# Scale rows and the later softmax-sum rows through DRAM instead of TensorE transposes

## The reference

```
f  = b[:, ::2, ::2]                       # 40 x 40 positions, 64 channels
w  = 3x3 patches of f                     # L = 1600 patches of 576 values
wn = w / max(norm(w), 1e-4)
y  = einsum('pd,ld->lp', w, wn) * mm      # 1600 x 1600 scores; mm is 1 where the mask patch is 0
y  = softmax(10 * y, axis = l) * mm
out = fold(einsum('lp,ld->pd', y, 4x4 patches of b)) / 4
```

## Time and profile before

| what | value |
|---|---|
| time, median of 3 runs | 1434.59 us (1431.02 to 1434.99) |
| time of the profiled execution | 1435.39 us |
| its span, first to last instruction | 1433.6 us |
| PE busy | 1327.2 us, 93% of the span |
| DVE busy | 1183.3 us, 83% |
| ACT busy | 857.9 us, 60% |
| DMA packets on SP's queue (q1) | 140.50 MB, 41.7% of 16 engines' span |
| mean granted PE clock | 0.983 |

### The profile page before, as it was taken

The page is one execution under the profiler, slowest core; times in us unless marked ns, Lnnn a source line. Parts: engine busy times, 40 slices in busy tenths (PEclk is TensorE's granted clock), DMA queues, the critical chain, the costliest instruction groups (busy, mean ns, idle before and its releaser), DMA issues.

```text
span 1433.6 us, 24384 instructions
## 1 busy us (share of the span) xinstructions
PE 1327.2 (93%) x7190; PEld 894.6 (62%) x7190; DVE 1183.3 (83%) x2827; ACT 857.9 (60%) x2233; POOL 46.9 (3%) x62
## 2 busy tenths in 40 slices
PE   4988999999999899999999899999999999998886
PEld 4756765676556665577656676567655766566433
DVE  3667889799888898889897888979987898978983
ACT  2677646676557565586565764666655855658331
POOL 1000000010000100001000000001000010000100
PEclk9997999999999999999999999999999999999998
DMA  5502482145822556135741359224572236313442
GB/s 91 89 1 85 109 173 76 47 116 119 163 64 67 124 113 150 49 86 127 143 117 33 104 118 179 70 52 110 126 156 67 71 107 135 94 32 96 131 136 53
DMA packets 180471, 142.54 MB, mean 99 GB/s; under 512 B 119859, under 2 KB 177267, under 8 KB 180339
## 3 DMA queue, kind: packets, MB, share of 16 engines
q1 hardware_dynamic: 180178, 140.50, 41.7%
q10 hardware_dynamic: 160, 0.49, 0.2%
HBM read 19.76 MB, written 13.11 MB: 23 GB/s over the span
## 4 chain that ended last, share of the span: by engine, by line
PE 54%; DVE 15%; ACT 11%; issue 8%; SPq 7%; DMA 5%; DVEq 0%; POOL 0%; ACTq 0%; POOLq 0%
PE psO L521 26%; PE psG L471 23%; SPq L326 4%; DVE G L968 4%; ACT S L697 4%; DVE Z L1001 3%; DMA SH<-G 3%; PE psG L480 3%; DVE S L898 3%; ACT G L708 2%; ACT G L683 2%; DVE G L979 2%; DMA SHJ<-G 2%; SPq L270 1%; ACT SQ L624 1%
## 5 line engine op out<-in xcount | busy, mean ns | idle before, releaser
L521 PE MATMUL psO<-Z,B 123*128 123x492 f32 (+2 forms) x1792 | 718.6, 530 | 46.0 <-DVE Z L1001 31.4
L521 PEld LDWEIGHTS psO<-Z,B 123*128 123x128 f32 x1792 | 325.8, 194 | 247.6 <-issue 133.8
L471 PE MATMUL psG<-LH,HL 128*123 128x246 f16 (+2 forms) x2616 | 407.2, 285 | 3.7 <-ACT G L670 3.0
L697 ACT ACTIVATE S<-S,nm 123x480 f32<-123x480 f32 (+3 forms) x560 | 308.5, 555 | 161.2 <-DVE nm L905 160.8
L471 PEld LDWEIGHTS psG<-LH,HL 128*123 128x123 f16 x2616 | 277.4, 137 | 125.4 <-issue 64.5
L708 ACT ACTIVATE G<-G,nb 123x492 f32<-123x492 f32 (+1 forms) x448 | 265.0, 639 | 60.3 <-DVE G L968 59.9
L898 DVE CUSTOM_DVE_ANT_0 S<-G,RB 123x492 f32<-123x492 f32 (+1 forms) x448 | 268.4, 604 | 25.8 <-ACT G L683 15.6
L979 DVE TENSOR_TENSOR G<-G,SH 123x492 f32<-123x492 f32 (+1 forms) x448 | 247.6, 591 | 48.9 <-DMA SH<-G 48.3
L968 DVE SCALAR_TENSOR_TENSOR G<-G,RA,psB 123x492 f32<-123x492 f32 (+1 forms) x448 | 270.4, 647 | 0.0
L883 DVE TENSOR_TENSOR G<-G,psG 123x492 f32<-123x492 f32 (+2 forms) x272 | 135.0, 496 | 90.4 <-PE psG L471 46.5
L1001 DVE TENSOR_TENSOR Z<-G 123x984 f32<-123x984 f32 (+2 forms) x192 | 197.2, 1028 | 0.0
(11 more groups left out here) (79 smaller groups left out, 575.8 us busy)
## 6 DMA issues: line engine op xcount, KB each, us to landing
SH<-G SPq DMA_DIRECT2D x336, 214.8 KB
SH<-G SPq DMA_DIRECT2D x112, 89.2 KB
SH<-G SPq DMA_DIRECT2D x336, 19.2 KB
XP<-x SPq DMA_DIRECT2D x20, 280.0 KB, 5.7
XP<-mid SPq DMA_DIRECT2D x20, 280.0 KB, 5.5
HL<-LH SPq DMA_DIRECT2D x16, 246.5 KB, 4.5
mid<-OSB SPq DMA_DIRECT2D x48, 80.0 KB, 2.3
out<-OSB SPq DMA_DIRECT2D x48, 80.0 KB, 2.3
```

What stands on the lines that cost most here:

```text
L471: last = pe.matmul(psG[0:TW, bank, b0 * TW:b1 * TW], st[:, v % 2, p:p + TW], mv[:, v % 2, lo:lo + n], start=i == 0, stop=i == len(terms) - 1)
L521: last = pe.matmul(psO[:, b, 0:n], B[:, o:o + 128], Z[:, 2 * (s % 2) + j, 0:n], start=t == 0, stop=t == TILES - 1)
L697: last = act.activation(y, y, ACT.Exp, bias=nm[:, k * TILES + t:k * TILES + t + 1], accum_out=sg[:, c:c + 1])
```

## The change

Only unit 0's first 8 scale blocks and the first 8 log-sum-exp blocks of each unit (groups 0 and 1) are still spread by PE. All else is written to DRAM as one row and read back with the source row repeated for 123 partitions.

- For the scales of unit w: PE transposes the 123 x 14 column once (slot 22), ACT copies the 14 x 123 result to `RT` (slot 23), SP writes it to `scale_row` in DRAM (slot 24) and reads it back onto 123 partitions in four DMAs, one for each score chunk: chunks 0 and 1 in slots 26 and 28, chunks 2 and 3 in slots 4 and 10 of the next body.
- For the last 6 log-sum-exp blocks of unit u: one transpose (slot 2), one ACT copy to `LT` (slot 2), a DRAM write (slot 3), one DMA of 123 x 738 into the new SBUF tile `LB` (slot 5). The arguments of chunks 2 and 3 then read `LB` in place of `psB`.
- Unit 0's two remaining spreads go to different banks. DVE no longer makes the separate column `R`.

```diff
+            def write_scales(w):
+                sp.wait_ge(scales_copied, w + 1)
+                sp.dma_start(scale_row[w].rearrange("(t p) -> t p", p=TW), RT[:, :]).then_inc(scales_out, 16)
+            def load_scales(w, k):
+                t0, n = S_CHUNKS[k]
+                if w == 0:
+                    if t0 + n <= RFIRST:
+                        return
+                    n, t0 = t0 + n - max(t0, RFIRST), max(t0, RFIRST)
+                else:
+                    sp.wait_ge(max_made, (w - 1) * NB + (k + 1) * TILES)
+                    sp.sem_inc(sp_gate, 1)
+                sp.wait_ge(scales_out, (w + 1) * 16)
+                row = scale_row[w:w + 1, t0 * TW:(t0 + n) * TW]
+                sp.dma_start(RB[:, t0 * TW:(t0 + n) * TW], row.to_broadcast([TW, n * TW])).then_inc(scales_in[k], 16)
+            def write_lse(u):
+                sp.wait_ge(lse_copied, u + 1)
+                sp.dma_start(lse_tail[u].rearrange("(t p) -> t p", p=TW), LT[:, :]).then_inc(lse_out, 16)
+            def load_lse(u):
+                sp.wait_ge(arg_made, u * NB)
+                sp.sem_inc(sp_gate, 1)
+                sp.wait_ge(lse_out, (u + 1) * 16)
+                sp.dma_start(LB[:, :], lse_tail[u:u + 1, :].to_broadcast([TW, LTAIL * TW])).then_inc(lse_in, 16)
 ...
                     if at and at[2] == 0:
                         shift_strip(at)
+                    if s == FIRST and u is None:
+                        write_scales(v)
+                    if s == 3 and u is not None:
+                        write_lse(u)
+                    if s == 5 and u is not None:
+                        load_lse(u)
+                    if s in (4, 10) and v is not None:
+                        load_scales(v, 2 if s == 4 else 3)
+                    if s == 24 and w is not None:
+                        write_scales(w)
+                    if s in (26, 28) and w is not None:
+                        load_scales(w, 0 if s == 26 else 1)
                     if s in (10, 11, 12) and w is not None:
                         lay_out_features(w, (("HL", "H1", "HV")[s - 10],))
 ...
+            def scale_rows(g):
+                pe.wait_ge(r_step, R_STEPS)
+                spread(psB[0:TW, g, :], RA, 4 * g, 4 * g + 4).then_inc(r_psum, 1)
+            def turn_scales(u, w):
+                pe.wait_ge(r_step, (w + 1) * R_STEPS)
+                pe.sem_inc(pe_gate, 1)
+                if u is not None:
+                    pe.wait_ge(arg_made, u * NB + 2 * TILES)
+                else:
+                    pe.wait_ge(r_rows, 2)
+                pe.transpose(psB[0:TILES, 1, 0:TW], RA[:, w * TILES:(w + 1) * TILES],
+                             idn[0:TW, 0:TW]).then_inc(scales_turned, 1)
+            def turn_lse(v, u):
+                pe.wait_ge(lse_dve, (u + 1) * LSE_STEPS)
+                pe.sem_inc(pe_gate, 1)
+                pe.wait_ge(b_made, (u + 1) * PAIRS)
+                pe.transpose(psM[0:LTAIL, 0:TW], lse[:, LHEAD:TILES], idn[0:TW, 0:TW]).then_inc(lse_turned, 1)
 ...
-                    if s == 4 and v is not None:
-                        scale_rows(u, v, 2)
-                    if s == 18 and v is not None:
-                        scale_rows(u, v, 3)
-                    if s == 5 and u is not None:
-                        lse_row(u, v, 2)
-                    if s == 10 and u is not None:
-                        lse_row(u, v, 3)
 ...
-                    if w is not None and s in (25, 26):
-                        scale_rows(u, w, s - 25)
 ...
+                row = psB[0:TW, k, 0:n] if k < 2 else LB[:, c0 - LHEAD * TW:c0 - LHEAD * TW + n]
 ...
-                                             in1=psB[0:TW, k % 2, 0:n],
+                                             in1=row,
```

More of the change, by code:

```diff
@@ L29 @@
 NK = len(P_CHUNKS)
+RFIRST = 8
+LHEAD = 8
+LTAIL = TILES - LHEAD
 SLOTS = NK * PAIRS
@@ L82, in contextual_attention @@
     mid = nc.dram_tensor("mid", (IMAGES, C, SIDE, SIDE), F32, kind="Internal").ap()
+    scale_row = nc.dram_tensor("scale_row", (UNITS, TILES * TW), F32, kind="Internal").ap()
+    lse_tail = nc.dram_tensor("lse_tail", (UNITS, LTAIL * TW), F32, kind="Internal").ap()
     with ExitStack() as ctx:
@@ L104, in contextual_attention @@
         SQ = sb("SQ", [128, FROWS // 2 * TW], F32)
+        RT = sb("RT", [TILES, TW], F32)
+        LT = sb("LT", [LTAIL, TW], F32)
+        LB = sb("LB", [TW, LTAIL * TW], F32)
         RB = sb("RB", [TW, TILES * TW], F32)
@@ L164, in contextual_attention @@
         r_rows = sem("r_rows")
+        scales_turned = sem("scales_turned")
+        scales_copied = sem("scales_copied")
+        scales_out = sem("scales_out")
+        scales_in = [sem(f"scales_in{k}") for k in range(NK)]
+        lse_turned = sem("lse_turned")
+        lse_copied = sem("lse_copied")
+        lse_out = sem("lse_out")
+        lse_in = sem("lse_in")
         norm_cols = sem("norm_cols")
@@ L197, in contextual_attention @@
         stored = sem("stored")
-        R_STEPS = 10
+        R_STEPS = 9
         LSE_STEPS = 12
@@ L390, in row_squares @@
                 pe.sem_inc(pe_gate, 1)
-                if v is not None:
-                    pe.wait_ge(r_rows, v * 4 + 3)
+                if v:
+                    pe.wait_ge(b_made, v * PAIRS)
                 for r in range(FROWS // 2):
@@ L408, in spread @@
                 return last
-            def scale_rows(u, v, g):
-                pe.wait_ge(r_step, (v + 1) * R_STEPS)
-                if u is not None:
[L414 to L422, removed]
@@ L426, in lse_row @@
+            def turn_lse(v, u):
[3 more added lines that the diff above has]
+                pe.transpose(psM[0:LTAIL, 0:TW], lse[:, LHEAD:TILES], idn[0:TW, 0:TW]).then_inc(lse_turned, 1)
+            def lse_row(v, k):
                 pe.wait_ge(lse_dve, v * LSE_STEPS + (LSE_STEPS // 2 if k == 0 else LSE_STEPS))
                 pe.sem_inc(pe_gate, 1)
[L428 to L431, removed]
+                if k == 1:
+                    pe.wait_ge(scales_copied, min(v + 2, UNITS))
+                elif v == 0:
+                    pe.wait_ge(r_rows, 1)
@@ L432, in lse_row @@
                 else:
-                    pe.wait_ge(arg_made, v * NB + (k - 1) * TILES)
+                    pe.wait_ge(arg_made, (v - 1) * NB + (k + 1) * TILES)
                 s0, n = P_CHUNKS[k]
-                spread(psB[0:TW, k % 2, :], lse, s0, s0 + n).then_inc(lse_rows, 1)
+                spread(psB[0:TW, k, :], lse, s0, s0 + n).then_inc(lse_rows, 1)
             def block_group(v, w, g):
@@ L445, in block_group @@
                     pe.wait_ge(r_step, w * R_STEPS + 4)
-                else:
-                    pe.wait_ge(r_rows, v * 4 + 3)
+                elif v:
+                    pe.wait_ge(b_made, v * PAIRS)
                 for t in (2 * g, 2 * g + 1):
@@ L551, in body @@
                     if s == FIRST and u is not None:
-                        lse_row(u, v, 1)
+                        lse_row(u, 1)
+                        turn_lse(v, u)
                     if pairs and not first:
@@ L561, in body @@
                     if s == 24 and v is not None:
-                        lse_row(v, w, 0)
+                        lse_row(v, 0)
                     if w is not None:
@@ L567, in body @@
                             band_sums(v, w)
+                    if s == 22 and w is not None:
+                        turn_scales(u, w)
                     if v is not None and 21 <= s < SLOTS - 1:
                         block_group(v, w, s - 21)
-                    if w is not None and s in (25, 26):
-                        scale_rows(u, w, s - 25)
             pe.wait_ge(mask_step, 2)
@@ L586, in _ @@
             band_sums(None, 0)
-            scale_rows(None, 0, 0)
-            scale_rows(None, 0, 1)
+            scale_rows(0)
+            scale_rows(1)
+            turn_scales(None, 0)
             body(None, 0, 1)
@@ L631, in roots, with scale_rows, copy_scales, copy_lse @@
                 act.activation(root[:, :], lnn[:, :], ACT.Exp, scale=0.5).then_inc(root_made, 1)
[L633 to L636, removed]
+            def scale_rows(g):
+                act.wait_ge(r_psum, g + 1)
+                act.activation(RB[:, 4 * g * TW:4 * (g + 1) * TW], psB[0:TW, g, 0:4 * TW], ACT.Copy).then_inc(r_rows, 1)
+            def copy_scales(w):
+                if w:
+                    act.wait_ge(scales_out, w * 16)
+                    act.sem_inc(act_gate, 1)
+                act.wait_ge(scales_turned, w + 1)
+                act.activation(RT[:, :], psB[0:TILES, 1, 0:TW], ACT.Copy).then_inc(scales_copied, 1)
+            def copy_lse(u):
+                if u:
+                    act.wait_ge(lse_out, u * 16)
+                    act.sem_inc(act_gate, 1)
+                act.wait_ge(lse_turned, u + 1)
+                act.activation(LT[:, :], psM[0:LTAIL, 0:TW], ACT.Copy).then_inc(lse_copied, 1)
             def block_group(u, v, g):
@@ L766, in body @@
                         softmax_pair(at)
```

(34 more changed lines are left out.)

3 lines of the change are left out of this document (removed).

## The result

The changed kernel takes 1449.3 us in the median of 4 runs (1445.68 to 1453.31), the kernel before 1432.8 us (1426.91 to 1434.99). The ratio is 1.0126, 95% interval 1.0092 to 1.0159: slower by 1.3%. That is 18 us by the ratio (13 to 23) and 16.5 us between the medians. The forecast was 1445 us, slower. One run of the whole study is in the chip's slower state, 1945 us at a mean granted PE clock of 0.66, of the kernel that splits only the load of slot 10; neither its time nor its trace is used.

A forecast was written before the change was run, and what follows sets the result against it. Two nearly equal limits: PE's work and a loop of DVE, ACT, SP and DMA. Lasting gains 3.8 us, losses 13.9 us: 1435.4 + 10.1 = 1445.5 us, stated as 1445 us; range 1428 to 1476 us.

The forecast's parts named there:

- The engines of a load: Each of the five new 123-partition loads runs on 3 engines, 41 rows each: 4.2 us, or 6.3 us for log-sum-exp.
- rival 1: New loads use all 16 engines, each taking 0.8 to 1.2 us and hidden: 1427 us, faster; chance 0.15.
- Rival 3: Three engines and slow DRAM reads, loads taking 8.3 and 12.4 us: 1508 us; chance 0.13.
- the 3 us a period: Slot 5: if the log-sum-exp load takes 12.4 us, the shift behind it would be 3 us late.
- Slot 4: Score chunk 2's load delays the pair shift and strip behind it, for which DVE waits: 1.2 us in each of 7 periods.
- 4.3 - 0.8 us of gains: Slots 4 and 5: 4.3 us of removed spreads, and slot 2's 0.8 us new transpose, both fall out of the sum.
- Slot 5: The log-sum-exp load, 6.3 us, follows the strip; the next shift still lands in time: hidden, 0.
- the last body: Slots are only 3.5 to 5 us, so the shift behind the 6.3 us log-sum-exp load comes late: about +2 us.
- Slot 10: Some 2 of the load's 4.2 us are worked off before the strip, which comes about 0.5 us late each period.
- The gain on PE: Spreads removed from PE's part of the chain give 8.1 us, less 0.8 us for the new transpose in slot 2.
- the 0.64 us for the shared bank: Opening: the second spread no longer waits for ACT's copy of the first in the same bank, gaining 0.64 us.
- PE, ACT and waits: New transposes, ACT copies and waits: counted 0, at worst a tenth of a us for each of 9 waits per unit.

The follow-up runs named there:

- The split version: The changed kernel with each of the five loads onto 123 partitions issued as two DMAs, of 112 and 11 partitions: 1429.08 us, ratio 0.9982.
- the kernel before with hidden loads: The kernel before plus loads of the same sizes and slots that nothing reads, each issued as 112 and 11 partitions: 1432.84 us, ratio 1.0012.
- The unread loads: The kernel before, all spreads kept, plus loads of the same sizes and slots into tiles nothing reads, each one 123-partition DMA: 1448.06 us, ratio 1.0118.
- 113 + 10: The changed kernel with each of the five loads issued as two DMAs, of 113 and 10 partitions: 1552.81 us, ratio 1.0863.

## Why the prediction came out right

**The engines of a load.** Predicted: 3, from the count of small packets in the opening. Shown by the packet counts (3, 16 + 11, 1 + 10, 16) and by the three packets in flight behind a load. The Trainium skill's rule (page "DMA: Bandwidth & Descriptors", section "Why a DMA increments its semaphore by 16 and not by 1") is the largest number up to 16 that divides the slowest dimension of both sides, here the partitions. It holds in these runs for 10, 11, 112, 113, 123 and 128, also where the source is one repeated row. So rival 1 (all 16 engines) is out. Rival 3 (slow reads) is out with 19 GB/s per engine. (Its sum also left out the 3 us a period that the prediction itself gives slot 5 at the slow rate; nothing came to hang on it.)

**Slot 4.** Predicted 7 x 1.2 = 8.4 us, and besides it the loss of 4.3 - 0.8 us of gains. Splitting that load gave 8 us back (3 to 13). In the traces the stretches from the strip sum of slot 27 to that of slot 6 add up to 262.9 us over the seven periods, and to 254.6 us with this load split. In size, and in the strip as the carrier, the 8.4 us stand, but at most six periods make them, not seven.

**Slot 5.** Predicted: hidden in the seven periods, 2 us in the last body. Measured 4 us, with an interval that holds 2 and also 0. Whether the last body pays is not shown. The part behind the last strip sum of slot 27 is 1.8 us longer than before, but it differs by as much between kernels for other reasons: 117.6 us where only slot 4's load is split, 119.5 us with all loads on 128 partitions.

**Slot 10** is the term that was mis-sized: predicted 7 x 0.5 = 3.5 us, measured 12 us (6 to 17). I let 2 of the 4.2 us be worked off before the strip and took DVE's wait as the cost. The trace has DVE waiting 1.6 to 2.9 us for this strip in five of the seven periods (2.18 us in the row above), and 2.2 us in a sixth, where the view names PE. The window's mean share of 0.92 is no idle time for the three engines behind a load. Part of it is caught up: from the strip sum of slot 13 to that of slot 20 the seven periods add up to 297.8 us, against 305.2 us before. So of the 11.5 us that the stretches in front of slot 13 are longer, a part is won back; how much of that belongs to slot 10 is not settled, since the kernel that splits slot 10 alone has no trace to read.

**The gain on PE** was oversized. Predicted 8.1 - 0.8 = 7.3 us if all loads were hidden. The split version is 2.6 us under the kernel before (0.6 to 4.7), or 4.3 us under the kernel before with hidden loads. In the opening none of the 0.64 us for the shared bank came. Here is the piece of the chain, before (its middle is in the earlier trace rows) and after:

```profile
25.01 1.20 PE psB L406 x4
...
28.05 7.52 PE psG L471 x66
```

```profile
24.73 2.02 PE psB L463 x8
...
26.78 0.59 ACT RB L696
...
27.42 0.37 PE psB L480
27.79 12.13 PE psG L538 x132
```

From the first spread to the first score matmul it is 3.04 us before and 3.06 us after: the spreads no longer wait for a bank, but the new transpose of the scales waits for ACT's second copy. That PE starts 0.26 us sooner comes from DVE, which no longer makes `R` and lets the spreads start 0.28 us sooner; the prediction had put that at 0. Why the rest of PE's gain is missing (that DVE, SP and the image loads end last just behind it) is argued from the chain and not tested.

**PE, ACT and waits** were counted at nothing. The unread loads have none of the new waits on PE, ACT and DVE and lose as much, so gain and new waits together come to about nothing on 3 engines. Each by itself is not shown.

**Luck in the number.** The sum had losses of 13.9 us and gains of 3.8 us, 10 us in all. The unread loads lose 17 us, and no gain is to be seen. Both errors go the same way, so the forecast of the change was some 40% short, though the direction and the mechanism held. It ended only 4 us under the median measured in part because it started from a kernel before of 1434.6 us, which is 1432.8 us in the four runs of the result.

## What to carry to other kernels

In every shape counted here a DMA from SP ran on the largest number of engines up to 16 that divides its partitions. Before a transfer of 123 partitions goes on a queue that others wait on, cut it into 112 + 11, or make the tile 128 tall. The price of a narrow transfer is not its bytes but the next small transfer behind it; look there, at what slack its reader has, and at how full the queue is at that place. And count the completions in the trace of before: the number of engines could be read from 23 small packets, before anything was built.

## What the runs showed that was not expected

- One partition can cost 124 us: 112 + 11 gave 1429 us and 113 + 10 gave 1553 us, with the same bytes and the same number of DMAs (and, with 113 + 10, a granted PE clock lower by 0.03).
- When a few engines have long queues, SP is held while it issues. In the 113 + 10 kernel SP's share of the chain is 22%, against 6% with 112 + 11, though its instructions are the same: the two issues of a log-sum-exp load took 7.65 us, against 0.75 us.
- The same loads in the same slots cost DVE no wait at the strip sums of slots 6 and 13 in the seventh period, which has no features to load or copy.
- Repeated reads of one 2952 B row of DRAM ran at 19 GB/s per engine, as fast as rows moved inside SBUF (about 19 GB/s by the earlier trace rows).
